# Cutting one write and six loads per turn into single parts, and sending the row of maxima from ScalarE's queue

## What is computed

```python
# layer 0: channel gate, then spatial gate
y  = conv1d(mean(x, (2, 3)), w_c)                    # over channels, 5 taps
yc = sigmoid(x * y[:, :, None, None])
sa = sigmoid(conv2d(concat([mean(yc, 1), max(yc, 1)]), w_s))   # 5 x 5
x  = yc * sa + x
# layer 1: attention
xn  = groupnorm(x, 32 groups) * gn_w + gn_b
q, k, v = split(einsum('bchw,oc->bohw', xn, qkv_w) + qkv_b)
attn = softmax(einsum('bndi,bndj->bnij', q, k) / 4)  # 256 x 256 per head
out  = einsum('bnij,bndj->bndi', attn, v)
return x + einsum('bchw,oc->bohw', out, proj_w) + proj_b
```

## Time and profile before

| | us |
|---|---|
| median of 3 runs (lowest, highest) | 199.0 (196.49, 199.06) |
| the profiled execution | 195.77 |
| its span, first to last instruction | 193.9 |
| busy: PE, DVE, ACT, POOL | 168.6, 142.1, 122.6, 112.2 |

### The profile page before, as it was taken

One profiled execution on the slowest core, in us unless ns is written; L12 is line 12 of the kernel. 1 busy time (PEld: TensorE's weight loads), 2 busy tenths in 40 slices (PEclk: granted clock), 3 DMA queues, 4 the chain that ended last, 5 costly groups with the idle time before them and its releaser, 6 DMA issues.

```text
span 193.9 us, 4752 instructions
## 1 busy us (share of the span) xinstructions
PE 168.6 (87%) x1515; PEld 105.4 (54%) x1518; DVE 142.1 (73%) x295; ACT 122.6 (63%) x250; POOL 112.2 (58%) x214
## 2 busy tenths in 40 slices
PE   7698985986959999989999998999999898888881
PEld 2265674453546667565656666576666655453320
DVE  0947769256743998888989897897989679797353
ACT  3073540451537797968878696977879686657760
POOL 5991282858473948678686968679784370101110
PEclk9969999999996999999999999999999999999999
DMA  3940302779397684637485755736676574600011
GB/s 100 358 111 19 108 3 83 167 221 210 84 227 163 165 202 122 158 119 167 148 172 144 194 126 145 162 124 148 194 177 129 154 163 125 176 28 3 28 32 54
DMA packets 19558, 26.24 MB, mean 135 GB/s; under 512 B 3756, under 2 KB 16468, under 8 KB 19540
## 3 DMA queue, kind: packets, MB, share of 16 engines
q1 hardware_dynamic: 18960, 25.47, 51.1%
q10 hardware_dynamic: 580, 0.55, 1.1%
HBM read 17.35 MB, written 8.42 MB: 133 GB/s over the span
## 4 chain that ended last, share of the span: by engine, by line
PE 34%; DMA 23%; SPq 20%; DVE 7%; POOL 6%; ACT 5%; issue 5%; POOLq 0%; ACTq 0%
DMA ks<-parts_dram 18%; SPq L256 11%; PE bank L667 7%; PE bank L693 7%; SPq L257 6%; PE bank L679 5%; PE bank L703 3%; DMA parts_dram<-parts 3%; PE bank L606 3%; DVE negmax L546 2%; SPq L244 2%; ACT pt L408 2%; PE bank L722 2%; DMA con<-consts 2%; PE bank L713 1%
## 5 line engine op out<-in xcount | busy, mean ns | idle before, releaser
L546 DVE TENSOR_REDUCE negmax<-bank 128x2 bf16<-128x512 f32 x128 | 86.1, 683 | 27.4 <-PE bank L667 24.9
L408 ACT ACTIVATE pt<-bank 128x512 f32<-128x512 f32 x128 | 73.5, 592 | 19.1 <-PE bank L679 18.9
L667 PE MATMUL bank<-ks,qs 96*128 96x256 bf16 x256 | 49.9, 276 | 11.3 <-DMA ks<-parts_dram 8.9
L679 PE MATMUL bank<-qs,ks 97*128 97x256 bf16 x256 | 49.2, 274 | 2.1 <-ACT pt L408 2.0
L667 PEld LDWEIGHTS bank<-ks,qs 96*128 96x128 bf16 x256 | 20.5, 101 | 38.5 <-DVE negmax L546 23.6
L693 PE MATMUL bank<-pt,vs 128*32 128x256 f32 x512 | 34.0, 383 | 0.1
L333 POOL TENSOR_TENSOR rest<-z,parts 128x512 f32<-128x512 f32 x15 | 17.4, 1158 | 27.5 <-ACT z L417 14.8
L679 PEld LDWEIGHTS bank<-qs,ks 97*128 97x128 bf16 x256 | 24.3, 98 | 8.2 <-ACT pt L408 4.6
L306 POOL TENSOR_TENSOR xall<-yo,xall 128x256 f32 (+1 forms) x15 | 10.9, 726 | 26.0 <-ACT yo L428 25.9
L693 PEld LDWEIGHTS bank<-pt,vs 128*32 128x32 f32 x512 | 14.8, 110 | 12.3 <-issue 3.4
L703 PE MATMUL bank<-xn,wall 128*128 128x256 f32 x64 | 20.0, 400 | 1.0 <-ACT xn L400 0.9
(11 more groups left out here) (70 smaller groups left out, 216.1 us busy)
## 6 DMA issues: line engine op xcount, KB each, us to landing
parts_dram<-parts SPq DMA_DIRECT2D x16, 384.0 KB, 2.6
qs<-parts_dram SPq DMA_DIRECT2D x16, 192.0 KB, 3.7
ks<-parts_dram SPq DMA_DIRECT2D x16, 192.0 KB, 4.0
xall<-x SPq DMA_DIRECT2D x4, 512.0 KB, 5.9
qs<-parts_dram SPq DMA_DIRECT2D x16, 128.0 KB, 3.9
ks<-parts_dram SPq DMA_DIRECT2D x16, 128.0 KB, 3.8
out<-xall SPq DMA_DIRECT2D x16, 128.0 KB, 2.2
gate<-gate_dram SPq DMA_DIRECT2D x6, 256.0 KB, 4.1
```

The lines of the kernel that those rows point to most:

```text
L408: nc.scalar.activation(pt[:, (u + LEAD) % UNITS, :, :].rearrange("p t n -> p (t n)"), st_bank[u % 2][:, :], ACT.Exp, scale=SCALE).then_inc ...
L546: nc.vector.tensor_reduce(negmax[:, slot(1), column:column + TILES], s_bank[u % 2][:, :].rearrange("p (t n) -> p t n", t=TILES), AX.X, ALU ...
L667: mm = pe.matmul(s_bank[u % 2][:, t * N:(t + 1) * N], qs[0:KQ, slot(1), h, a, t * P:(t + 1) * P], ks[0:KQ, slot(1), h, a, :], start=True, ...
L679: mm = pe.matmul(st_bank[u % 2][:, t * N:(t + 1) * N], ks[0:KQ + 1, slot(d), h, a, t * P:(t + 1) * P], qs[0:KQ + 1, slot(d), h, a, :], sta ...
```

## The change

The one write of three parts becomes three writes, each issued when its part is there (part 0 at `p1_ready`, part 1 and part 2 at their `split_step`), each with a semaphore of its own. The six loads become seven; each reads a single part of q or of k and writes it to one or more neighbouring blocks of 16 rows. The order of the blocks changes so that the six products stay the same (q blocks: part 0 three times, part 1 twice, part 2; k blocks: part 2, 0, 1, 1, 0, 0). A copy is now the outermost count of the source: `unsqueeze(0).broadcast_to([copies, HD, ...])`. The row of maxima is issued by ACT, behind its first exponential of the turn, and SP does not wait for `mrow_ready` any more. POOL gets a wait for `st_ready` ahead of part 2, PE's wait for the stacks counts 7 x 16 = 112.

```diff
-        parts_out, stack_in = sem("parts_out"), [sem(f"stack_in{r}") for r in range(RING)]
+        parts_out, stack_in = [sem(f"parts_out{i}") for i in range(3)], [sem(f"stack_in{r}") for r in range(RING)]
...
             def turn(k, slot, has, lap):
-                if has(0):
-                    wait(sp, mrow_ready, k + 1)
-                    sp.dma_start(qs[KQ:KQ + 1, slot(0), :, :, :].rearrange("p h a (t n) -> p (h a t) n", t=TILES),
-                                 maxrow[:, slot(0), :]).then_inc(mrow_in, 16)
-
+                def stack(tile, g, part, first, copies):
+
+                    r = slot(2)
+                    rows = slice(first * HD, (first + copies) * HD)
+                    src = parts_dram[r, part, g, :, :].unsqueeze(0).broadcast_to([copies, HD, HEADS * 2 * N])
+                    sp.dma_start(tile[rows, r, :, :, :].rearrange("p h a n -> p (h a n)"), src).then_inc(stack_in[r], 16)
+
+                def part_write(part):
+                    r = slot(3)
+                    sp.dma_start(parts_dram[r, part].rearrange("g d (h n) -> (g d h) n", h=HEADS),
+                                 parts[:, r, part, :]).then_inc(parts_out[part], 16)
 
                 if has(2):
-                    r = slot(2)
-                    wait(sp, parts_out, 16 * (k + 3))
-                    for first, q_parts, k_part in ((0, 3, 0), (3, 2, 1), (5, 1, 2)):
-
-                        rows = slice(first * HD, (first + q_parts) * HD)
-                        src_q = parts_dram[r, 0:q_parts, 0, :, :].rearrange("s d n -> d s n")
-                        src_k = parts_dram[r, k_part, 1, :, :].unsqueeze(1).broadcast_to([HD, q_parts, HEADS * 2 * N])
-                        sp.dma_start(qs[rows, r, :, :, :].rearrange("p h a n -> p (h a n)"), src_q).then_inc(stack_in[r], 16)
-                        sp.dma_start(ks[rows, r, :, :, :].rearrange("p h a n -> p (h a n)"), src_k).then_inc(stack_in[r], 16)
-
-
+                    wait(sp, parts_out[0], 16 * (k + 3))
+                    stack(qs, 0, 0, 0, 3)
+                    stack(ks, 1, 0, 1, 1)
+                    stack(ks, 1, 0, 4, 2)
+                if has(2):
+                    wait(sp, parts_out[1], 16 * (k + 3))
+                    stack(qs, 0, 1, 3, 2)
+                    stack(ks, 1, 1, 2, 2)
+                    wait(sp, parts_out[2], 16 * (k + 3))
+                    stack(qs, 0, 2, 5, 1)
+                    stack(ks, 1, 2, 0, 1)
                 if has(3):
-                    r = slot(3)
-                    wait(sp, split_step, 3 * (k + 4))
-                    sp.dma_start(parts_dram[r].rearrange("s g d (h n) -> (g d h) s n", h=HEADS), parts[:, r, :, :]).then_inc(parts_out, 16)
-
+                    wait(sp, p1_ready, k + 4)
+                    part_write(0)
                 if has(-3):
...
+                if has(3):
+                    wait(sp, split_step, 3 * (k + 3) + 2)
+                    part_write(1)
+                    wait(sp, split_step, 3 * (k + 4))
+                    part_write(2)
                 stands_in(aside, k, 2)
...
+                    wait(pool, st_ready, UNITS * k)
                     wait(pool, split_step, 3 * (k + 3) + 2)
                     nc.gpsimd.tensor_tensor(parts[:, r, 2, :], rest[:, :], parts[:, r, 1, :], ALU.subtract).then_inc(split_step, 1)
...
+                    if u == 0 and has(0):
+                        wait(act, mrow_ready, k + 1)
+                        act.dma_start(qs[KQ:KQ + 1, slot(0), :, :, :].rearrange("p h a (t n) -> p (h a t) n", t=TILES),
+                                      maxrow[:, slot(0), :]).then_inc(mrow_in, 16)
                     if u == 0 and has(3):
                         wait(act, z_ready, k + 4)
-                        wait(act, parts_out, 16 * k)
+                        wait(act, parts_out[0], 16 * k)
...
                     if u == 0:
-                        wait(pe, stack_in[slot(1)], lap(1) * 96)
+                        wait(pe, stack_in[slot(1)], lap(1) * 112)
```

## The result

The changed kernel takes 304.1 us in the median (302.08 to 306.14, 4 runs) against 198.05 us before (4 runs, one more than in the table ahead). The ratio is 1.537 (95% interval 1.518 to 1.555). Forecast were 283 us and slower, with 250 to 345 as the range. Some executions of a kernel are 1 to 4% longer at a lower granted clock: the medians here are of all executions, the ratios of the others alone.

The account below looks back on a forecast made before the run. Bound before: narrowly the 8.5 us ring through SP, maxima and stacks, PE close behind. After: first stacks at 44.7, fifteen 14.0 us turns, 24.9 us to the end, 1.9 around it: 281.5, leaned to 283 us; range 250 to 345.

Parts of the forecast that it names:

- The form of the loads: Part and stack loads: with the copy outermost, four of seven run on 3, 2, 2 and 2 engines, not 16.
- The rate of one engine: Stack loads: each confined DMA engine moves 23.1 GB/s, as in the loads of x.
- The end of 14.4 GB/s: Slower engine rate, from a stretch of part loads: 19.1 us of drain, 395 us in all; chance 0.07.
- the drain: Seven loads of a pair: the busiest engine needs 11.9 us for 67 rows, more than PE's 8.3 us.
- The fixed part: Each turn, on top of the loads: part 0's write 0.35 us, then receipt, issue and next start 1.7 us.
- the tail: From the last stacks to the end of the span: 23.9 us as now, plus 1.0 us for a lower clock.
- The lean of half of 3.2 us: Added because the median of the runs was 3.2 us over the profiled execution: 281.5 became 283 us.
- Rival D: Part 0's write gets in ahead of the loads: a turn of 11.9 us, 250 us in all; chance 0.05.
- The row on ACT: Row of maxima on ACT's queue: ring cut, at most 11.3 us gained; 0.54 us issue hidden, landing in 1.7 us harmless.
- POOL's wait: Part 2 waits for unit 3's transposed scores, which stand earlier: covered by 0.7 us.
- The signs: Expected profile: chain mostly DMA and SP, PE waiting near 5.5 us a turn, DMA share near 0.3 or less.
- Rival A: Loads spread over all 16 engines after all: 8 us gained by the cut ring, 188 us; chance 0.06.

Follow-up runs that it names:

- the 40, 54 and 67 rows: Rows on the busiest DMA engine per pair: changed kernel with two loads confined (238.6 us), with three (276.3 us), and as it is (304.1 us).

## Why the prediction was right, point by point

**The form of the loads.** Right, and the whole of it: the form alone turns 198.6 into 330.6 us, its removal takes 304 back to 197. The reading from three missing landing times, a thin basis, was borne out by the arrivals (61 for a pair) and by the share of 0.13. The rule of the Trainium skill ("DMA: Bandwidth & Descriptors", "Why a DMA increments its semaphore by 16 and not by 1") agrees with this. That the few engines are the same from load to load shows in the 40, 54 and 67 rows and in the two trains of rows at the end of every drain.

**The rate of one engine.** Taken as 23.1 GB/s from the x loads. Measured are 25.5 in the window, 26.1 from 0.157 us a row and 27.5 by the slope. The end of 14.4 GB/s fell, as argued: in the packets the median row takes 0.16 us here and 0.30 us in the kernel before, where 16 engines pull at once.

**The mis-sized term: the drain.** I took 11.9 us for the 67 rows. By the packets, from the start of a pair's first row to the end of its last it is 13.0 us (mean of 14 turns). The rate was taken too low, not too high: at 0.157 us the 67 rows would be 10.5 us. Some 2.5 us come on top that the sum put at nothing: in the turn shown 39 of the first 96 rows took over 0.25 us and up to 1.02, in the first 5 us, while the other loads, the store and two writes move too. Two errors of opposite sign thus made the 11.9 look better than it was, which is luck. The fixed part was nearly right: 2.05 us forecast, measured 0.8 us from the last row to the next issue, write and receipt in it, and 1.5 us from the issue to the first row, 2.3 us. Both together are the 1.4 us by which the turn is 15.37 and not 14.0: 1.1 in the drain, 0.3 in the fixed part.

The sum, term by term: first stacks 47.07 us against 44.7 (+2.4), fifteen turns of 15.37 against 14.0 (+20.5), the tail 304.0 - 277.6 = 26.4 against 24.9 (+1.5), in all 24.4 us of span: 279.6 becomes 304.0. The lean of half of 3.2 us towards a slower median had the wrong sign here: the profiled execution took 305.85 us, the median is 304.1. Rival D, the fixed part hidden, did not happen by itself. With the writes on ACT's queue it did, and gave back 2.5 us a turn; the turn was then 12.86 us and not D's 11.9, for the same reason as above.

**The row on ACT.** The issue was 0.51 to 0.60 us, hidden, as said. "The row lands in 1.7 us: nothing" was wrong: 6.3 us, and PE waits for it for 18.8 us in 13 waits:

```profile
PE bank L693 <- DMA qs<-maxrow: 18.8, 13, 2.4
```

It costs nothing in the sum only because PE has some 3.6 us to spare a turn even so. With spread loads ahead of it the row lands in 2.3 us.

**POOL's wait** cost 0.8 us in total; **SP's issues** were hidden, as said. The clock was 0.83 over a turn, and 0.50, that is 1.2 GHz, where PE came back from its wait, as forecast.

**The signs.** DMA and SP head the chain, SP waits for the write ahead of its loads, and the DMA share is 0.28, as said. Two signs came out otherwise: the loads of 16 rows have no time to landing, and PE's wait at the scores is 3.4 to 3.6 us in the two turns shown and not 5.5, since it waits for the row of maxima as well (1.85 us).

**Rival A**, had it held, would have come out at or slightly above the 188 us I put on it: with all engines at work the changed kernel takes 192 us with twelve loads and 189.6 with nine. No run had seven spread loads.

## What to carry to other kernels

Look at a transfer's outermost count before its size: a repeat or a part put outermost can leave most of the DMA engines idle, and a missing time to landing in the list of issues is the sign (it then misses for all transfers that count on the same semaphore). A confined transfer costs twice: by its own drain, 13.0 of 15.4 us here, and by what stands behind it on its queue, 8 packets of a write on each engine, for which the next loads wait. And when several changes are made at once, undo them apart: the loads of single parts, which help, were hidden by the place of one count in an access pattern.

## What the runs showed that I had not expected

- A load on 3 engines slows the small transfer that another engine issues right behind it on its own queue: 4.7 to 6.3 us to landing in place of 2.3, because of 3 of its 16 pieces.
- One load on 3 engines, 25 rows on the busiest, costs a turn of 11.5 to 11.7 us, as much as two loads on 2 engines with 40 rows (11.35).
